# Seven-layer attention kernel on one core: value rows copied straight into the value weights with two transfers in place of four, and the rope products at another place on VectorE

## The reference

```python
def rope(t, offset, head_dim):
    ...
    rot = jnp.concatenate([-t2, t1], axis=-1)
    return t * cos + rot * sin
...
h = rmsnorm(x, norm_w)
q = (h @ Wq.T).reshape(B, Td, H, D)
kv = (encoder_out @ Wkv.T).reshape(B, Te, 2, H, D)
k, v = (kv[:, :, 0], kv[:, :, 1])
q = rope(q, decoder_offset, D)
k = rope(k, 0, D)
scores = jnp.einsum('bqhd,bkhd->bhqk', q, k) * scale
attn = jax.nn.softmax(scores, axis=-1)
out = jnp.einsum('bhqk,bkhd->bqhd', attn, v).reshape(B, Td, d)
out = out @ Wo.T
return residual + out
```

## Time and profile before

| | before |
|---|---|
| median of 3 runs | 2307.22 us (2305.52 to 2307.72) |
| profiled execution, own time | 2310.75 us |
| its span | 2308.9 us |
| PE busy | 2109.8 us, 91% of the span |
| PE weight loads | 1719.6 us, 74% |
| DVE busy | 1866.1 us, 81% |
| ACT busy | 1646.2 us, 71% |
| POOL busy | 1234.6 us, 53% |
| queue of SP's transfers | 279.80 MB, 49.1% of 16 engines' span |
| granted clock of PE, mean | 0.986 |

### The profile page before, as it was taken

One profiled execution on the slowest core, in us unless ns is written; L12 is line 12 of the kernel. 1 busy time (PEld: TensorE's weight loads), 2 busy tenths in 40 slices (PEclk: granted clock), 3 DMA queues, 4 the chain that ended last, 5 costly groups with the idle time before them and its releaser, 6 DMA issues.

```text
span 2308.9 us, 100596 instructions
## 1 busy us (share of the span) xinstructions
PE 2109.8 (91%) x40685; PEld 1719.6 (74%) x40685; DVE 1866.1 (81%) x4849; ACT 1646.2 (71%) x3280; POOL 1234.6 (53%) x3173
## 2 busy tenths in 40 slices
PE   2789988999999998999999999899999999899986
PEld 2577777877887776788788777787788777677775
DVE  3578888988778888888787888898877888888863
ACT  0367766888887775788888776688888776578874
POOL 3354434776555433677565443477655543366743
PEclk6899999999999999999999999999999999999999
DMA  6355555555555555555555555555555444555541
GB/s 149 92 131 129 128 130 137 127 128 129 132 129 128 128 126 131 131 130 124 131 134 126 125 130 129 138 126 132 123 133 130 118 118 113 132 131 132 121 99 49
DMA packets 310570, 289.17 MB, mean 125 GB/s; under 512 B 50080, under 2 KB 251552, under 8 KB 310112
## 3 DMA queue, kind: packets, MB, share of 16 engines
q1 hardware_dynamic: 305120, 279.80, 49.1%
q10 hardware_dynamic: 4128, 1.65, 0.4%
q0 software_dynamic: 864, 1.28, 0.3%
HBM read 130.51 MB, written 34.60 MB: 72 GB/s over the span
## 4 chain that ended last, share of the span: by engine, by line
PE 60%; DVE 16%; ACT 6%; SPq 5%; issue 5%; DMA 5%; DVEq 2%; POOL 0%; POOLq 0%; ACTq 0%
PE ps_turn L898 9%; PE ps_scores_t L844 8%; PE ps_scores L797 8%; PE ps_turn L828 8%; PE ps_wide L926 7%; DVE row_max L1159 5%; PE ps_turn L903 3%; SPq L533 3%; PE ps_wide L923 3%; PE ps_wide L874 3%; PE ps_wide L873 3%; PE ps_wide L880 3%; DMA k_slots<-k_dram 3%; DVEq L1102 2%; DVE shifted L1165 2%
## 5 line engine op out<-in xcount | busy, mean ns | idle before, releaser
L1159 DVE TENSOR_REDUCE row_max<-ps_scores 128x16 f32<-128x1024 f32 x448 | 544.5, 1215 | 252.6 <-PE ps_scores L797 134.5
L1165 DVE TENSOR_TENSOR shifted<-ps_scores,row_max 128x512 f32<-128x512 f32 x896 | 598.5, 685 | 15.3
L738 ACT ACTIVATE probs<-ps_scores_t 128x512 f32<-128x512 f32 x896 | 486.3, 595 | 83.2 <-PE ps_scores_t L844 81.1
L728 ACT COPY pv_sb<-ps_turn 128x256 f32<-128x256 f32 x448 | 167.0, 373 | 350.6 <-PE ps_turn L828 347.0
L797 PE MATMUL ps_scores<-k_slots,qk_rows 32*64 32x256 f32 x7168 | 309.6, 401 | 48.3 <-DMA k_slots<-k_dram 45.0
L828 PEld LDWEIGHTS ps_turn<-probs,v_ones 128*32 128x32 f32 x14336 | 221.2, 110 | 151.6 <-issue 81.1
L844 PE MATMUL ps_scores_t<-ident,shifted 64*128 64x64 f32 x7168 | 320.6, 230 | 13.7 <-DVE attn L1177 9.5
L844 PEld LDWEIGHTS ps_scores_t<-ident,shifted 64*128 64x128 f32 x7168 | 259.3, 139 | 57.8 <-ACT turned L709 10.8
L828 PE MATMUL ps_turn<-probs,v_ones 128*32 128x64 f32 x14336 | 293.9, 222 | 4.5 <-ACT turned L709 0.8
L709 ACT COPY turned<-ps_turn 128x256 f32<-128x256 f32 (+2 forms) x470 | 192.7, 410 | 106.9 <-PE ps_turn L961 78.9
L602 POOL TENSOR_TENSOR mlp_var_eps<-mlp_mean_var,eps 128x1 f32<-128x1 f32 x128 | 24.3, 190 | 431.7 <-DVE mlp_mean_var L1103 431.7
(11 more groups left out here) (170 smaller groups left out, 4324.5 us busy)
## 6 DMA issues: line engine op xcount, KB each, us to landing
v_ones<-v_rows SPq DMA_DIRECT2D x1792, 64.0 KB, 2.4
k_slots<-k_dram SPq DMA_DIRECT2D x448, 256.0 KB
k_dram<-qk_rows SPq DMA_DIRECT2D x448, 64.0 KB
x_in<-in_x SPq DMA_DIRECT2D x64, 64.0 KB, 2.1
ctx_in<-in_ctx SPq DMA_DIRECT2D x64, 64.0 KB, 2.0
out<-x SPq DMA_DIRECT2D x64, 64.0 KB, 2.2
k_dram<-zeros SPq DMA_DIRECT2D x4, 256.0 KB, 8.7
w<-in_L_xattn_W SPq DMA_DIRECT2D x2, 256.0 KB, 6.6
```

Of the source, the lines that this page charges most:

```text
L738: nc.scalar.activation(probs[:, b, :, :], ps_scores_t[:, b, :] .rearrange("p (h t) -> p h t", t=LEN), ACT.Exp, scale=SCALE).then_inc(probs ...
L1159: v.tensor_reduce(row_max[:, :].rearrange("p (g n) -> p g n", n=SLOTS), ps_scores[:, :, 0:256].rearrange("p g (n k) -> p g n k", k=LEN), A ...
L1165: v.tensor_tensor(shifted[:, j % 2, u, :].rearrange("p (g n k) -> p g n k", n=SLOTS, k=LEN), ps_scores[:, 2 * u:2 * u + 2, 0:256].rearrang ...
```

## The change

1. `v_pairs` takes the tile as an argument. ACT copies v from PSUM straight into `v_ones`. In it the blocks with b = e are then where they belong; the two blocks with b = 1-e lie on the wrong half of the partitions.
2. A new ACT copy `v_rows_out` copies v from `v_ones` to `v_rows` in every phase, behind the copy of the turned tiles (in layer 2 behind `copy_rope_v`) and ahead of the gelu.
3. SP sends only the two blocks that must change partitions, from `v_rows`. This is a function of its own, `v_out`, which waits for the new copy and is called one phase later, between `spread` and `rows_out`.
4. The parts of `v_ones` that stay constant are set by six more memsets in the setup.
5. Where a phase holds rope products and an up part, the products stand between the residual and the second `shift`, not behind the post-norm work.

```diff
-        v_landed = [signal(f"v_landed{c}", 64, FAR) for c in range(FAR)]
+        v_landed = [signal(f"v_landed{c}", 32, FAR) for c in range(FAR)]
...
                     sp.dma_start(k_rows(c)[:, K_HOME:], qk_rows[:, c, 1, :]).then_inc(k_written[c].sem, 16)
-                    if rope:
-                        sp.wait_ge(rope_v_ready.sem, rope_v_ready.at(r, j))
-                    else:
-                        sp.wait_ge(rows_ready.sem, rows_ready.at(r, j))
+
+                def v_out(r, j):
+
+                    f = j % FAR
+                    sp.wait_ge(v_rows_ready.sem, v_rows_ready.at(r, j))
                     for e in range(2):
-                        for b in range(2):
-                            sp.dma_start(v_ones[64 * e:64 * e + 64, f, b, :, :], v_rows[64 * b:64 * b + 64, f, e, :, :]) \
-                                .then_inc(v_landed[f].sem, 16)
+                        b = 1 - e
+                        sp.dma_start(v_ones[64 * e:64 * e + 64, f, b, :, :], v_rows[64 * b:64 * b + 64, f, e, :, :]) \
+                            .then_inc(v_landed[f].sem, 16)
...
                 def phase(r, j):
                     if exists(r, j + QKV - 1):
                         spread(r, j + QKV - 1)
+                        v_out(r, j + QKV - 1)
                     if exists(r, j + QKV):
                         rows_out(r, j + QKV)
...
+                def v_rows_out(r, j):
+
+                    ready = rope_v_ready if layer_of(j) == L1_CROSS else rows_ready
+                    act.wait_ge(ready.sem, ready.at(r, j))
+                    nc.scalar.copy(v_pairs(v_rows, j % FAR), v_pairs(v_ones, j % FAR)).then_inc(v_rows_ready.sem, 1)
...
                         copy_rope_v(r, j + QKV)
+                    if exists(r, j + QKV):
+                        v_rows_out(r, j + QKV)
                     if has_mlp(r, j - UP):
                         gelus(r, j - UP)
...
                         v.memset(v_rows[:, :, e, :, at:at + HD], value).then_inc(setup_mem, 1)
+                        v.memset(v_ones[:, :, e, :, at:at + HD], value).then_inc(setup_mem, 1)
...
                         residual(r, j - OUT)
+                    if rope and has_mlp(r, j - UP):
+                        rope_products(r, j + QKV)
                     if exists(r, j) and not late:
                         shift(r, j, 1)
...
-                    if rope:
+                    if rope and not has_mlp(r, j - UP):
                         rope_products(r, j + QKV)
```

More of the change, by code:

```diff
@@ L329, in build @@
         rope_v_ready = signal("rope_v_ready", {L1_CROSS: 1})
+        v_rows_ready = signal("v_rows_ready")
         post_rstd = signal("post_rstd", {n: 3 for n in POST_NORM})
@@ L358, in k_rows, with v_pairs @@
             return k_dram[c, 0:P * K_ROW].rearrange("(p x) -> p x", x=K_ROW)
-        def v_pairs(f):
-            wide = v_rows[:, f, :, :, :]
+        def v_pairs(tile, f):
+            wide = tile[:, f, :, :, :]
             step = wide.ap[1][0] + HD
@@ L507, in setup_psum @@
             return bank[:, (n % 4) * P:(n % 4 + 1) * P]
-        N_MEM = 13
+        N_MEM = 19
         STORED_0 = 1
@@ L518, in rows_out @@
                 def rows_out(r, j):
-                    c, f = j % RING, j % FAR
+                    c = j % RING
                     rope = layer_of(j) == L1_CROSS
@@ L716, in copy_rows @@
                         .then_inc(rows_ready.sem, 1)
-                    nc.scalar.copy(v_pairs(j % FAR), ps_wide[:, V_COLS].rearrange("p (e h d) -> p e h d", e=2, d=HD)) \
+                    nc.scalar.copy(v_pairs(v_ones, j % FAR), ps_wide[:, V_COLS].rearrange("p (e h d) -> p e h d", e=2, d=HD)) \
                         .then_inc(rows_ready.sem, 1)
@@ L722, in copy_rope_v @@
                     act.wait_ge(qkv_ready.sem, qkv_ready.at(r, j))
-                    nc.scalar.copy(v_pairs(j % FAR), ps_scores_t[:, 1, 0:P].rearrange("p (e h d) -> p e h d", e=2, d=HD)) \
+                    nc.scalar.copy(v_pairs(v_ones, j % FAR), ps_scores_t[:, 1, 0:P].rearrange("p (e h d) -> p e h d", e=2, d=HD)) \
                         .then_inc(rope_v_ready.sem, 1)
```

## The result

| | before | changed |
|---|---|---|
| median | 2307.47 us (2305.52 to 2313.65, 4 runs) | 2288.21 us (2282.01 to 2288.79, 4 runs) |
| ratio, 95% interval | | 0.9905 [0.9885, 0.9926] |
| profiled execution, own time | 2310.75 us | 2288.3 us |
| PE wait before the scores for `k_slots` | 45.0 us, 50 times | 50.3 us, 57 times |
| K write, median landing | - | 2.2 us |

The kernel became faster by 0.95%, 19 us, where the forecast said 50. All of the gain is in the phases with rope products; the other half of the forecast, in the stretches without MLP parts, did not come. (In line names, L808 is the scores, L934 the start of `mlp_up`, L542 the read back, L527 the K write, L535 the transfers of v.)

The account below looks back on a forecast made before the run. PE has 60% of the chain; the change can reach its waits for k_slots (45.0 us) and rope products (31.3 us). Terms -26 - 25 - 4 + 5 = -50 us from 2307.2 give 2257 us, range 2238 to 2288.

Parts of the forecast that it names:

- Rope products first: Phases with rope products and an up part: products ahead of the second shift let mlp_up start earlier, -26 us.
- SP's list: 67 phases without MLP parts: two of six issues go, a turn falls from 4.48 to 4.1 us, -25 us.
- L: Landing time of the K write in SP's queue, taken as 2.2 us; a turn was to cost L + 1.92 us.
- floor of six steps: SP's queue before the change: a turn of its list costs at least six issue steps, 3.85 us.
- The start: Between 47 and 113 us: the read back goes as soon as the K write has landed, -4 us.
- The extra ACT copy: ACT, up phases outside rope: the new copy delays gelu and the copy of pv, +5 us; free in down phases.
- K lands no faster: Rival on SP's queue: L near 2.5 to 2.6, turn as long as before, 2284 us (2271 to 2292), chance 0.22.
- the slower rival: Rival outside the stretches: SP's new wait for the K write becomes the bound, 2351 us at L = 3.1, chance 0.05.

Follow-up runs that it names:

- the other list of SP: Kernel before with only the v part of the change, its two transfers issued behind the K write, rope products at their old place: 2280.34 us, 0.986.
- The kernel with four transfers: Changed kernel with all four transfers of v sent from v_rows between read back and K write: 2691.88 us, 1.1644 of the kernel before.

## Why the prediction was wrong, step by step

*Rope products first, -26 us: right.* The 40 phases with rope products and an up part took 249.8 us before and 225.2 after, from one unit's scores to the next, 24.6 less (6.25 to 5.63 each); the part alone gave 0.9%, and 24 us again on top of the other list of SP.

*SP's list, -25 us: wrong, it is 0.* This is the step that failed. L was right: the K write lands after 2.2 us in the median (2.4 in the mean of the stretches), and an even turn takes L + 1.92 = 4.1. The fault is the 4.48 from which it was subtracted. 4.1 is the length of a turn in which nothing is disturbed; 4.48 is the mean over turns of which many are. By the prediction's own floor of six steps, 3.85, and by the 3.71 of the timeline, an even turn was shorter before. Like with like, by the same sorting as above: without an instruction packet 3.99 us before (23 turns) and 4.11 after (24), with one 4.90 (44) and 4.86 (43); in the median the undisturbed turn even grew, from 3.70 to 4.09. Neither kind got clearly shorter. In the disturbed turns after, the three issue steps took 2.43 us, not 1.92, and the landing 2.43, not 2.19. The rows that should have warned were there: the first issue of v in the earlier trace rows took 1.50 us of the 4.74 of its turn, where an even one takes 0.60; the sum took such stretches for a part of the six issues that would go with two of them. Most stayed: an issue of over 0.9 us stands in 38 of the 67 turns before and in 27 after.

Before, four issues of v stood behind the K write, in the shadow of its landing, and with 2.4 us they outlasted it in most phases (SP had to wait for the landing only 33 times); the change cut two of them and took the other two out of the shadow, 1.24 us that now stand in a row with 2.2 us of landing. With the two in the shadow, the stretches took 272.0 and 268.6 us in place of 299.4: cutting two issues was worth what the forecast said, and a little more, and the move ahead of the K write cost it all again. The prediction set a rule against its own forecast, from the Trainium skill's page "DMA: Bandwidth & Descriptors", section "Rules for kernel authors": issue early, compute, wait late. The page speaks of compute in the shadow; here other issues stood there, and the runs agree with the rule in this form.

*The start, -4 us: right in sign, a third in size.* The first read back is issued 1.57 us after its K write, 2.85 before, which is 1.3 us gained, once. From the scores of unit 0 to those of unit 16 nothing came: 54.89 us, 54.81 before. (The scores of unit 16 start at 110.05 us, 112.26 before; the rest of these 2.2 us is the first K write, which came 0.85 us earlier, and in kernels with the same loads ahead of it lies anywhere from 49.6 to 51.8 us.)

*The extra ACT copy, +5 us: too dear.* It takes 0.30 us. Alone it costs nothing that can be told, 3 us at the most; in the changed kernel the phases with a down part, where the forecast had it free, together grew by 2.8 us of 748, and those with an up part not at all. With v behind the K write, and the same copy, the down phases took 747.9 us, so these 2.8 are not the copy's.

*The rivals.* The time came out at the second's, 2284 by "K lands no faster", but not by its mechanism: K did land in 2.2 us. It said that SP's turn would stay as long as before, which it did, but for another reason; that the time fell on its 2284 is luck. What the slower rival described, a landing with nothing issued in its shadow, is there in every phase (SP waits for the K write 447 times); at L = 2.2 it stays under the pace of the phases with MLP parts, so it did not decide. The kernel with four transfers is the slower rival in full: its turn, L + 5 steps or 5.0 us even when undisturbed, is above the 4.94 us of an average phase.

*What was to be seen.* The wait for `k_slots` was to fall to 10 to 25 us and rose to 50.3; the chain in the stretches was to hold hardly any issue of v and holds 10 to 21%. PE's wait for the rope product was to be 5 to 6 us and is 2.7, the phases with it 5.6 and are 5.63. Issues of v 896 and queue bytes 279.80 to 221.02 MB are as forecast; ACT is busy for 91 us more, not 121 (0.27 a copy; overlap with its predecessor makes the busy time grow by less).

## What to carry to other kernels

Subtract like from like: if a model gives the length of an undisturbed turn, take an undisturbed turn of the trace as its other side, and let the disturbed ones carry over; a modelled best case against a measured mean shows a gain that is not there. In an issuing queue that waits for one of its own transfers, an issue between the wait's end and the next transfer waited for is paid in full, and one behind that transfer is free as long as the landing covers it: put the awaited transfer first and as many of the others behind it as fit. Here two fit (1.1 us of issues under some 2.3 of landing) and four (2.4 us) did not: halving their number behind the K write gained 32 us, and halving it while moving them ahead gained none.

## What was not expected of the hardware

A transfer issued by POOL holds POOL for 0.54 to 0.57 us, as long as an issue holds SP (0.56 to 0.60), so moving an issue to a compute engine only moves the cost. A single row of 16 KB went out as 16 packets of 1024 bytes and 16 of 4 bytes, one of 64 bytes as 32 of 4 bytes. The mean granted clock is 0.986 in some executions and 0.996 in others without a difference in time: the runs of the changed kernel at 0.996 and 0.986 took 2288.79 and 2288.12 us. The profiled ones differ in the first 57 us, where PE is busy for only 15 to 17: the granted clock there is 0.66 in the changed kernel and 1.00 in the one with v behind the K write. Within one group a lower clock does go with a longer time: the kernel before took 2304.7 to 2307.3 us at 0.987 and 2315.8 and 2316.7 at 0.979 and 0.978. A single issue of SP sometimes took 0.9 to 1.9 us in place of 0.6, in the changed kernel each time beside a packet of an instruction queue on the transfer engines; that the packet holds it is likely by the times of their ends, but not shown by an experiment.
